# Layer 1's attention and output stage as one stage, by pairs of neighbouring query tiles

## The reference

```
for each of the two layers:
    h = layernorm(x) * (1 + ca) + sa
    x = x + ga * attention(h)
    h = layernorm(x) * (1 + cb) + sb
    x = x + gb * ffn(h)
```

```
qkv = x @ w_qkv.T ; q, k, v = split(qkv)
attn = softmax(causal(q @ k.T * 128**-0.5))
out = (attn @ v) @ w_out.T + b_out
```

## Time and profile before

| | us |
|---|---|
| median of three executions | 2284.77 |
| the profiled execution | 2283.89 |
| its span, first to last instruction | 2282.1 |
| PE busy | 2114.3 (93%) |
| DVE busy | 1758.6 (77%) |
| ACT busy | 1551.3 (68%) |
| POOL busy | 654.6 (29%) |

### The profile page before, as it was taken

One profiled execution on the slowest core, in us unless ns is written; L12 is line 12 of the kernel. 1 busy time (PEld: TensorE's weight loads), 2 busy tenths in 40 slices (PEclk: granted clock), 3 DMA queues, 4 the chain that ended last, 5 costly groups with the idle time before them and its releaser, 6 DMA issues. The chain is left out here.

```text
span 2282.1 us, 45663 instructions
## 1 busy us (share of the span) xinstructions
PE 2114.3 (93%) x16684; PEld 927.0 (41%) x16684; DVE 1758.6 (77%) x4030; ACT 1551.3 (68%) x3249; POOL 654.6 (29%) x1219
## 2 busy tenths in 40 slices
PE   6799999999999999999999999999999698989983
PEld 5143333333333333333333333333332287567731
DVE  3888888888888888888888888888885277244477
ACT  2078787877878787878787787878787445146633
POOL 2214142332313232414233231313211044000077
PEclk8599999999999999999999999999999799999955
DMA  5230312222121303031222212130200300000001
GB/s 150 41 63 11 67 25 52 38 39 50 27 50 32 65 12 71 10 67 24 54 38 40 50 27 50 32 64 8 45 2 2 103 0 0 1 1 2 1 28 46
DMA packets 129528, 84.74 MB, mean 37 GB/s; under 512 B 90273, under 2 KB 119073, under 8 KB 129313
## 3 DMA queue, kind: packets, MB, share of 16 engines
q1 hardware_dynamic: 129312, 81.91, 18.2%
HBM read 26.81 MB, written 16.78 MB: 19 GB/s over the span
## 5 line engine op out<-in xcount | busy, mean ns | idle before, releaser
L755 ACT ACTIVATE probs<-b_bank 128x512 f32<-128x512 f32 (+1 forms) x2304 | 1171.8, 578 | 347.2 <-PE b_bank L915 336.1
L632 DVE TENSOR_REDUCE m_part<-a_bank 128x1 f32<-128x512 f32 (+3 forms) x2048 | 1190.5, 634 | 153.1 <-PE a_bank L885 111.0
L915 PE MATMUL b_bank<-q_pack,k_pack 34*128 34x512 bf16 (+7 forms) x5120 | 920.8, 348 | 4.4 <-DMA q_pack<-m_rows 2.9
L885 PE MATMUL a_bank<-k_pack,q_pack 64*128 64x512 bf16 (+3 forms) x2560 | 811.1, 357 | 54.3 <-DVE m_part L632 30.7
L957 PE MATMUL acc<-probs,v_tile 128*32 128x512 f32 (+3 forms) x5120 | 586.7, 539 | 3.1 <-POOL probs L498 0.8
L915 PEld LDWEIGHTS b_bank<-q_pack,k_pack 34*128 34x128 bf16 (+1 forms) x5120 | 310.6, 94 | 511.9 <-ACT probs L755 436.3
L885 PEld LDWEIGHTS a_bank<-k_pack,q_pack 64*128 64x128 bf16 x2560 | 226.0, 94 | 343.7 <-DVE m_part L632 209.7
L498 POOL TENSOR_SCALAR_AFFINE_SELECT probs<-probs 128x512 f32<-128x512 f32 (+1 forms) x192 | 151.7, 790 | 609.7 <-ACT probs L755 609.6
L629 DVE CUSTOM_DVE_ANT_0 a_bank<-a_bank,mask_a 128x128 f32<-128x128 f32 (+3 forms) x512 | 241.8, 512 | 66.7 <-PE a_bank L885 66.7
L957 PEld LDWEIGHTS acc<-probs,v_tile 128*32 128x32 f32 x5120 | 107.8, 108 | 174.8 <-issue 117.8
L895 PE MATMUL a_bank<-future,pick 64*128 64x128 bf16 x1024 | 134.4, 219 | 0.0
(11 more groups left out here) (199 smaller groups left out, 1869.9 us busy)
## 6 DMA issues: line engine op xcount, KB each, us to landing
q_pack<-part SPq DMA_DIRECT2D x384, 64.0 KB, 2.3
k_pack<-part SPq DMA_DIRECT2D x192, 64.0 KB, 2.3
headT<-scratch SPq DMA_DIRECT2D x80, 128.0 KB, 4.0
scratch<-qkvT SPq DMA_DIRECT2D x16, 512.0 KB, 2.8
xg<-in_L_attn_x SPq DMA_DIRECT2D x16, 256.0 KB, 2.8
scratch<-qkvT SPq DMA_DIRECT2D x32, 128.0 KB, 2.7
q_pack<-m_rows SPq DMA_DIRECT2D x256, 2.0 KB
x<-in_L_attn_x SPq DMA_DIRECT2D x4, 1024.0 KB, 11.6
```

The costliest lines, as they stand in the source:

```text
L632: dve.tensor_reduce(out, bank[:, 0:w], AX.X, ALU.max).then_inc(a_maxed, 1)
L755: act.activation(probs[:, n % P_RING, h, at:C], b_bank[bank_no(("B", n, h))][:, at:C], ACT.Exp, scale=HD ** -0.5) \
L885: ins = pe.matmul(a_bank[at % A_RING][:, 0:w], q_pack[buf][rows, hp, 0, q:q + P], k_pack[buf][rows, 0, C * c:C * c + w], start=True, stop= ...
L915: ins = pe.matmul(b_bank[bank_no(slot)][:, at:at + C - q], k_pack[par][rows, n2, P * kt:P * (kt + 1)], q_pack[par][rows, h // 2, n2, C * j ...
```

## The change

`layer1_attention` and `layer1_out` become one function, `layer1`, and one block.

The tasks are now in quads: two neighbouring long tiles and two neighbouring short ones of the same batch element, interleaved as long, short, long, short. Two neighbouring tiles (256 rows) are a unit. There are 16 units, and all later work is by units. The first four quads' elements are 0, 0, 1, 1, so that the first eight tasks need only element 0; element 1's 12 fills are made in tasks 0 to 5, two in each (LATER), through the two turn banks.

The exponential is one instruction for a whole task, over up to four banks of PSUM, with one sum. The transposed probabilities of a unit lie side by side, 256 query columns for each key tile; v is the stationary operand and the result comes out transposed, so the transpose of the output goes away. It is copied to SBUF (take_ao), multiplied with w_out into the same out_bank (project), and DVE scales it by the inverted sum in the same instruction that adds the row's x.

x2 is now written to DRAM in `layer0_out` by SP (16 DMAs of 256 KB) and read back by units, in the natural order of rows, into a ring of six (xr). POOL adds the bias to it (add_bias). Its old place in SBUF holds the probabilities of the long units, and a part of attn's that of the short ones. The two layernorms follow by units with fixed lags: a step with lag L of unit r stands in the slot of its second task plus L. Lag 1: multiply, take_ao, add_bias; 2: project, add_attention, first deviation; 3: first centre, scale, add_offset; 4: add_shift, second deviation; 5: second centre, gain; 6: add_branch. The loop has N + 6 = 38 slots, unrolled. The additions of the bias, the offset and all gains are POOL's.

The diff, cut to its core:

```diff
@@ layer0_out, SP @@
+            for n in range(NB):
+                for b in range(B):
+                    sp.wait_ge(x2_made, 2 * n + b + 1)
+                    sp.dma_start(x2_rows[b].rearrange(...)[:, :, n, :], x2[:, n, b, :, :]).then_inc(x2_out, 16)
@@ layer1 (was layer1_attention and layer1_out) @@
-        TASKS = [(b, t) for big in range(NT - 1, NT // 2 - 1, -1) for b in range(B) for t in (big, NT - 1 - big)]
+        QUADS = [(0, 0), (0, 1), (1, 0), (1, 1), (0, 2), (0, 3), (1, 2), (1, 3)]
+        TASKS = [(b, t) for b, i in QUADS for t in (NT - 1 - 2 * i, 2 * i, NT - 2 - 2 * i, 2 * i + 1)]
+        UNITS_1 = [tuple(sorted((4 * q + s, 4 * q + s + 2), key=lambda u: TASKS[u][1])) for q in range(len(QUADS)) for s in range(2)]
+        X_RING = 6
+        H_RING = 4
+        UPFRONT = len(FILLS) // B
+        LATER = {u: range(UPFRONT + 2 * u, UPFRONT + 2 * u + 2) for u in range((len(FILLS) - UPFRONT) // 2)}
+        SLOTS = N + 6
+        for u in range(N):
+            TURNS += [("keys", before[u] + g) for g in range(chunks[u])] + [("fill", f) for f in LATER.get(u, ())]
+        def second_task(r):
+            return 4 * (r // 2) + r % 2 + 2
+        def due(v, lag):
+            return [r for r in range(NU) if second_task(r) + lag == v]
@@ SP @@
+            def load(r):
+                if r >= X_RING:
+                    sp.wait_ge(stored[r % X_RING], 16 * (r // X_RING))
+                sp.dma_start(xr[:, r % X_RING, :, :], rows(r, x2_rows)).then_inc(xr_in[r % X_RING], 16)
+            sp.wait_ge(x2_out, 16 * B * KV)
+            for r in range(X_RING - 1):
+                load(r)
+            for r in range(NU):
+                sp.wait_ge(res_made, r + 1)
+                sp.dma_start(rows(r, out), xr[:, r % X_RING, :, :]).then_inc(stored[r % X_RING], 16)
+                if r + X_RING - 1 < NU:
+                    load(r + X_RING - 1)
@@ PE @@
+            def multiply(r):
+                low, high = UNITS_1[r]
+                b, t = TASKS[low]
+                pe.wait_ge(taken, before[max(low, high) + 1])
+                if r:
+                    pe.wait_ge(x3_made, 2 * r)
+                for kt in range(t + 1):
+                    pe.matmul(out_bank[:, 0:2 * P], v1[:, b, kt, :], pT(r)[:, kt, :], start=kt == 0, stop=False)
+                pe.matmul(out_bank[:, P:2 * P], v1[:, b, t + 1, :], pT(r)[:, t + 1, P:2 * P], start=False, stop=True) \
+                    .then_inc(multiplied, 1)
+            def project(r):
+                b = TASKS[UNITS_1[r][0]][0]
+                pe.wait_ge(ao_taken, r + 1)
+                for k in range(2):
+                    ins = pe.matmul(out_bank[:, D * k:D * (k + 1)], aoT[:, r % 2, P * k:P * (k + 1)], woT[:, b, :], start=True, stop=True)
+                ins.then_inc(projected, 1)
+            for u in range(SLOTS):
+                if u < N:
+                    turn(u, 0)
+                    if u + 2 < N:
+                        score(u + 2)
+                    if chunks[u] > 1:
+                        turn(u, 1)
+                for r in due(u, 2):
+                    project(r)
+                if u < N:
+                    for g in range(2, chunks[u]):
+                        turn(u, g)
+                for r in due(u, 1):
+                    multiply(r)
+                for n in LATER.get(u, ()):
+                    wait_for_bank(("fill", n))
+                    fill(n, bank_of(("fill", n))[:, :])
@@ DVE @@
+            def add_attention(r):
+                dve.wait_ge(exped, max(UNITS_1[r]) + 1)
+                dve.reciprocal(rl[:, r, :], ls[:, r, :]).then_inc(inverted, 1)
+                dve.wait_ge(inverted, r + 1)
+                dve.wait_ge(xb_made, r + 1)
+                dve.wait_ge(projected, r + 1)
+                for k in range(2):
+                    dve.scalar_tensor_tensor(out=xr[:, r % X_RING, k, :], in0=out_bank[:, D * k:D * (k + 1)], scalar=rl[:, r, k:k + 1],
+                                             in1=xr[:, r % X_RING, k, :], op0=ALU.mult, op1=ALU.add).then_inc(x3_made, 1)
+                moments(0, r, xr[:, r % X_RING, :, :], x3_made, 2 * r + 2)
+            for u in range(SLOTS):
+                if u + 2 < N:
+                    maximum(u + 2)
+                for r in due(u, 2):
+                    add_attention(r)
+                for r in due(u, 4):
+                    add_shift(r)
+                for r in due(u, 6):
+                    add_branch(r)
+                (then the odd fills' copies of LATER)
@@ ACT @@
+            def exponential(u):
+                ...
+                act.activation(p1[:, u % 2, 0:w], region(u)[:, 0:w], ACT.Exp, bias=nm[:, u:u + 1], scale=INNER ** -0.5,
+                               accum_out=ls[:, r, k:k + 1]).then_inc(exped, 1)
+            exponential(0)
+            act.wait_ge(x2_out, 16 * B * KV)
+            for u in range(SLOTS):
+                if u < N:
+                    take(u, 0)
+                if u + 1 < N:
+                    exponential(u + 1)
+                for r in due(u, 3):
+                    if r >= H_RING:
+                        act.wait_ge(res_made, r - H_RING + 1)
+                    centre(0, r, hr[:, r % H_RING, :, :], xr[:, r % X_RING, :, :], hn_made)
+                for r in due(u, 5):
+                    centre(1, r, hr[:, r % H_RING, :, :], hr[:, r % H_RING, :, :], yn_made)
+                if u < N:
+                    for g in range(1, chunks[u]):
+                        take(u, g)
+                for r in due(u, 1):
+                    take_ao(r)
+                (then the even fills' copies of LATER)
@@ POOL @@
+            for u in range(SLOTS):
+                for r in due(u, 1):
+                    add_bias(r)
+                for r in due(u, 3):
+                    scale(r)
+                for r in due(u, 5):
+                    gain(r)
+                for r in due(u, 2):
+                    deviation(0, r)
+                for r in due(u, 4):
+                    deviation(1, r)
+                for r in due(u, 3):
+                    add_offset(r)
```

More of the change, by code:

```diff
@@ L1443, in _ @@
+            def project(r):
[4 more added lines that the diff above has]
+                ins.then_inc(projected, 1)
             score(0)
             score(1)
[L1445 to L1448, removed]
-                if g == 0 and u + 2 < N:
-                    score(u + 2)
-                if g == chunks[u] - 1 and u:
-                    turn_ao(u - 1)
@@ L1625, in centre, with take_ao @@
+            def take_ao(r):
+                act.wait_ge(multiplied, r + 1)
+                if r >= 2:
+                    act.wait_ge(projected, r - 1)
+                act.activation(aoT[:, r % 2, :], out_bank[:, 0:2 * P], ACT.Copy).then_inc(ao_taken, 1)
+            def centre(which, r, dst, src, done):
+                act.wait_ge(shift_made[which], r + 1)
                 for k in range(2):
-                    ins = act.activation(dst[:, b, k, :], src[:, b, k, :], ACT.Identity, bias=shift[:, which, b, k:k + 1],
-                                         scale=rs[:, which, b, k:k + 1])
+                    ins = act.activation(dst[:, k, :], src[:, k, :], ACT.Identity, bias=shift[:, which, r % 2, k:k + 1],
+                                         scale=rs[:, which, r % 2, k:k + 1])
@@ L1649, in _ @@
-            run(act, turn)
-        @block.tensor
-        def _(pe):
-            pe.wait_ge(consts, 4)
-            def turn(n, a, bb, c):
-                if a:
-                    for b in range(B):
-                        pe.wait_ge(staged, upto(2 * n + b + 1))
-                        wait_over(pe, x3_made, 2 * n + b - 1)
-                        for k in range(2):
-                            cols = bank[b][:, D * k:D * (k + 1)]
-                            pe.matmul(cols, ao[:, b, P * k:P * (k + 1)], woT[:, b, :], start=True, stop=False)
-                            ins = pe.matmul(cols, one[0:1, :], last_rows[0:1, 0, b, :], start=False, stop=True)
-                        ins.then_inc(projected, 1)
-            run(pe, turn)
+            exponential(0)
@@ new lines, in _ @@
+            act.wait_ge(x2_out, 16 * B * KV)
[15 more added lines that the diff above has]
+                    take_ao(r)
+                for n in LATER.get(u, ()):
+                    if n % 2 == 0:
+                        act.wait_ge(filled, n + 1)
+                        act.activation(into(FILLS[n]), bank_of(("fill", n))[:, :], ACT.Copy).then_inc(taken_a, 1)
```

396 lines of the change are left out of this document (135 added, 261 removed).

## The result

The changed kernel takes 2225.1 us (median of four, 2222.53 to 2226.67), the kernel before 2284.61 us on the same chip (2280.68 to 2285.26): a ratio of 0.9741, 95% interval 0.9726 to 0.9757, 59.5 us less. The forecast was 2224.

What follows compares the result with a forecast made beforehand. TensorE bounds the attention stage; the 117.6 us POOL-DVE-ACT output chain is laid beside it. Start, quads at 20.4 + 4.6 = 25 us and tail end the span at 2222.3, plus 1.8: 2224 us, range 2204 to 2252.

Steps and rivals of the forecast that it cites:

- no overlap: Rival: ACT waits for POOL at every centre, ahead of TensorE's copies; quads of 33.1 us, 2287 us in all; chance 0.06.
- TensorE's price of 20.4 us a quad: TensorE's own work in one quad: 34 tiles at 0.55 us, 18.7, and two unit projections of 0.85 us each.
- (b): TensorE waits for ACT's copies of chunks 1 and up, behind the small unit's centre: 1 us long rows, 2.5 short, 1.8.
- (c): The small unit's multiply waits for DVE's addition, behind the score row's mask, maximum and negation: stall 1.7 us a quad.
- The three stalls: TensorE's waits from in-order queues in a quad: for the exponential, ACT's copies and DVE's addition; sum 4.3 us.
- (a): Transposes wait for ACT's exponential behind take_ao and a copy: 1.6 us for the longest tiles, 0 for the last, mean 0.8.
- 3 us at the start: Slow clock after the first wait for an exponential: score row 6.26 us instead of 3.27; these 3 us kept in quad 0.
- The rival "clock": Rival: stalls bring TensorE to half clock once a quad, 3 us each, 21 us more, 2245 us; chance 0.12.
- the forecast's main case: 25 us a quad with granted clock 1.00 but at the start and the tail: 2224 us, own range 2214 to 2236, chance 0.53.
- The port: Rival: DVE additions held by POOL's large operations, half of 34 us on the path, 17 more, 2241 us; chance 0.11.
- The exponentials: One ACT instruction a task saves the fixed part of 48 of 80 instructions, counted at nothing; 0.107 us a tile over several banks.
- The tail: After the last small multiply, unit 15's layernorm chain behind unit 14's work queued on POOL: 17 us, last addition at 2219.5.

Runs made afterwards that it cites:

- the one with the projection first: Changed kernel with the big unit's projection issued before the score row two tasks ahead, and DVE's add_attention before that row's maximum: 2218.0 us, ratio 0.9722.
- the early exponential: Changed kernel with the exponential of a quad's second long task (from the second quad on) issued before the small unit's take_ao and the next copy: 2225.85 us, ratio 0.9753.

## Why the prediction was right

The mechanism was right and most of its terms were, but that the sum came within 1 us is in part luck. Quads 0 and 1 came out 2.2 us shorter and quads 2 to 7 2.0 us longer. And the four executions of the changed kernel lie 4 us apart. By its own steps, forecast against the profile after:

| step | forecast | measured |
|---|---|---|
| first score row | 1973.3 | 1973.83 |
| first transposes | 1982.1 | 1982.50 |
| quads 0 and 1 | 66.2 | 64.0 |
| quads 2 to 7 | 148.5 | 150.5 |
| end of the last long multiply | 2196.8 | 2197.0 |
| end of the last short multiply | 2202.5 | 2203.25 |
| last addition | 2219.5 | 2221.05 |
| end of the span | 2222.3 | 2224.1 |

*What bounds it.* Right: the POOL-DVE-ACT chain lies beside TensorE, and half of POOL's large operations gone change nothing. The "no overlap" case would have shown quads of 33 us; they have 24 to 26.

*TensorE's price of 20.4 us a quad.* Right: with (b) and (c) taken away the quads fall to 18.0 to 23.8 us, in the mean 21.1 (the first has the longer rows ahead, the last has none). In the changed kernel itself quads 2 to 7 take 150.5 us, of which TensorE waits 27.8: 20.4 to 20.5 a quad are left. Quad 0 was priced with eight fills and quad 1 with four; by these borders it is six and six, which leaves their sum as it is.

*The three stalls.* In quads 2 to 6 their sum was right, 3.8 to 4.4 us against 4.3, and their shares were not. (c), forecast 1.7, was 1.52 to 1.67. (b), forecast 1 for long rows and 2.5 for short, was 1.3, 1.8, 2.8, 2.7, 2.8, then 5.2 in the last quad, because there no score row stands before the copies; that took back more than the 1.5 us that I had subtracted for the rows that are missing. (a), forecast 0.8 in the mean, was 0.9, 0.5 and nothing: in quad 3 the next transposes began 2.5 us behind the end of the small multiply (2082.54 - 2080.00), not 3.0, and the other work was enough from quad 4 on. The experiments show (b) and (c) to be causes: taken away each alone they take 10.6 and 9.9 us of TensorE's idle time away, and together 20.1. With (a) taken away alone nothing is gained.

*The clock.* I kept 3 us at the start. That was mis-sized: the row that took 6.26 us has 16 key tiles and the one of 3.27 that I set against it 14, while a row of 16 tiles takes 3.60 us at full clock (that of 2034.53 in the profile after), so 2.7 were lost before. Now the place reads

```profile
1982.50 1.12 PE L1491 MATMUL turn_bank<-ident,p 128*128 128x128 f32 x4 [4.78 <-ACT p L1615]
1983.41 4.39 PE L1470 MATMUL score_banks<-qkT 128*128 128x512 f32 x8
```

The row has 15 tiles, for which 3.39 us is the time at full clock (that of 2046.79), and the transposes take 0.60 at other places: 1.0 and 0.5 us lost and not 3, which is most of what quads 0 and 1 are shorter. The rival "clock" is partly true. Quads 5 and 7 have a granted clock of 0.93 and 0.86, behind waits of 2.72 and 5.21 us; at quad 5 the four transposes behind it take 1.06 us instead of 0.60. It did not come at every quad: waits of 1.3 and 1.8 us left 1.00, and so did the two of 2.82 in quads 4 and 6. The Trainium skill (TensorE: Matmul & The Clock Gate, What's actually happening) has activity as what lifts the clock. The rows agree in part: each fall stands behind a wait, but not each wait has one behind it. Quad 6 shows it at one and the same place. The first two lines are of the changed kernel, the other two of the one with the projection first:

```profile
2164.69 0.63 PE L1491 MATMUL turn_bank<-ident,p 128*128 128x128 f32 x4 [2.82 <-ACT x L1624]
2165.15 1.67 PE L1470 MATMUL score_banks<-qkT 128*128 128x512 f32 x4
```
```profile
2152.43 1.09 PE L1491 MATMUL turn_bank<-ident,p 128*128 128x128 f32 x4 [2.82 <-ACT x L1634]
2153.31 3.19 PE L1470 MATMUL score_banks<-qkT 128*128 128x512 f32 x4
```

The same matmuls behind the same wait take nearly twice as long, and the quad is busy for 24.5 us instead of 21.4. So a kernel's time has a part of some us that its waits alone do not fix, and the forecast's main case had none for it inside the quads.

*The port.* The rival's 17 us did not come. DVE's additions are held at times (to 1.81 us against 0.68), but the 32 of them last 16.6 + 11.9 = 28.5 us in all, 7 more than at 0.67 each:

```profile
L1577 DVE TENSOR_TENSOR hr<-hr,rowmod 128x512 f32<-128x512 f32 x16 | 16.6, 1039 | 5.2 <-POOL hr L1697 5.2
...
L1584 DVE TENSOR_TENSOR xr<-xr,hr 128x512 f32<-128x512 f32 x16 | 11.9, 745 | 6.1 <-POOL hr L1707 6.1
```

The page SBUF — State Buffer of the Trainium skill (Who interferes with whom) says that the two engines hold each other up in such operations. The trace agrees, and it goes both ways. POOL's first small operation of a deviation takes 0.55 to 0.65 us beside DVE's add_branch, where it takes 0.20 alone:

```profile
2084.42 0.94 DVE L1584 TENSOR_TENSOR xr<-xr,hr 128x512 f32<-128x512 f32 x1
...
2084.76 0.65 POOL L1687 TENSOR_TENSOR ve<-mv,eps 128x2 f32<-128x2 f32 x1
```

That deviation is the one that ACT's centre of stall (b) waits for, in each of quads 2 to 7. So some 0.4 us a quad of the port are on the path, near the 0.3 that I held, though not by the additions that I had in mind. The run without half of POOL's large operations does not speak against it, since these small ones take 0.55 to 0.65 there too. No run takes this away alone.

*The exponentials.* The step "saves the fixed part of 48 of 80 instructions, on an engine with slack, so nothing by itself" failed: back in chunks, and with the reduction that goes with them, they cost 8.1 us, of which 4.0 are waits of TensorE and the rest slower matmuls. ACT has 14 of 24 us of work a quad, but TensorE waits for its exponential in (a) and at the start, and for DVE's addition, which the reduction delays, in (c). The sum came out right all the same, since I had priced the chain with the single exponential. Several banks in one instruction cost nothing extra: 1967 ns for 16 tiles, 1108 for 8, 684 for 4, which is 0.107 a tile.

```profile
L1615 ACT ACTIVATE p<-score_banks,nm 128x2048 f32<-128x2048 f32 x2 | 3.9, 1967 | 8.6 <-DVE nm L1547 8.6
...
L1615 ACT ACTIVATE p<-score_banks,nm 128x1024 f32<-128x1024 f32 x2 | 2.2, 1108 | 0.0
...
L1615 ACT ACTIVATE p<-score_banks,nm 128x512 f32<-128x512 f32 x2 | 1.4, 684 | 0.0
```

*The tail.* From the end of the last short multiply to the end of the last addition it is 17.8 us where I had 17, with the queue of unit 14 on POOL as I had it:

```profile
2213.38 0.19 POOL L1692 TENSOR_TENSOR shift<-minus,rs 128x2 f32<-128x2 f32 x1
2213.52 1.26 POOL L1702 TENSOR_TENSOR xr<-xr,last_rows 128x512 f32<-128x512 f32 x1
...
2214.77 1.26 POOL L1707 TENSOR_TENSOR hr<-hr,last_rows 128x512 f32<-128x512 f32 x1
2215.99 0.19 POOL L1687 TENSOR_TENSOR ve<-mv,eps 128x2 f32<-128x2 f32 x1
```

DVE had unit 15's statistics ready at 2213.54; its deviation begins at 2215.99, behind an offset and a gain. With the offsets left out the tail is as long (21.3 us to the end of the span, against 21.2), because the gain of unit 14, which waits for ACT's centre of that unit, still stands ahead. With scale, offset and gain of the last two units on DVE it is 19.5 and 19.7 us in the two versions that have this. On the chain that ends last POOL also has four small operations of 0.55 to 0.67 us beside DVE's additions, 1.8 us more than at 0.19 to 0.20 each; no run takes these away.

What stays open is what decides whether the clock falls behind a wait, and so how much of the slower matmuls (up to 6.9 us, in the version with all fills in front) belongs to an edit and how much to the one execution that was profiled.

## What to carry to other kernels

When a chain that is bound by latency is laid beside a stage that one engine bounds, price that engine's work first, and then walk one period of each in-order queue: each instruction that waits for another engine's late result holds back what stands behind it. Busy shares won't show this. Here ACT had 10 us of slack in 24 and still set 11 to 13 us of the time with the place of the centres in its queue. Look at the last period by itself, since the work that hides a wait is missing there.

When two edits of the same kernel are compared, take the time from where they begin to differ, and split the busiest engine's time into idle and busy. The idle time shows what the order of a queue does: there the two stalls added up to within 0.4 us, while the times alone left some 5 us open.

## What the runs showed of the hardware

How fast TensorE's matmuls are behind a wait in the middle of full work is not given by the length of that wait alone. Behind waits of 1.3 and 1.8 us the granted clock over the quad was 1.00, and behind one of 2.18 (the early exponential) and one of 2.72 (quad 5) it was 0.93. Behind 2.82 us in quad 6 it was 1.00 in the changed kernel and 0.87 in the one with the projection first, and behind 2.82 us in quad 4 it was 1.00 there and 0.87 in the one with all fills in front. A fall of that kind cost 3 us of TensorE's time (24.5 against 21.4 us busy, 22.8 against 19.8).

An fp32 exponential over up to four banks of PSUM costs the same per column as one over one bank: 1967 ns for 2048 columns, 1108 for 1024 and 684 for 512.
